# One-column writes behind GpSimd's scatters and gathers, weight bounds cut in four, and a last chunk in halves

## The reference, cut to what matters

```python
mod = (_silu(L0_c) @ L0_wmod).reshape(L0_c.shape[0], 6, 1, -1)
sa, ca, ga, sb, cb, gb = ...            # ga, gb: sign kept, size at least 0.25
h = _layernorm(x) * (1 + ca) + sa
x = x + ga * attention(h)               # linear attention with a memory term, d_mem 32
h = _layernorm(x) * (1 + cb) + sb
x = x + gb * moe(h)                     # 8 experts, top 2, gelu, 128 -> 512 -> 128

def moe(x):
    gate = softmax(flat_x @ w_gate.T)
    topk_scores, topk_idx = top_k(gate, 2)
    h = gelu(einsum('td,edh->teh', flat_x, W1) + b1)
    y = einsum('teh,ehd->ted', h, W2) + b2
    out = einsum('ted,te->td', y, cw)   # cw: the two scores at their experts
```

## Time and profile before

| | |
|---|---|
| median of 3 runs | 661.02 us |
| the profiled execution's own time | 661.97 us |
| its span | 660.2 us |
| busy: PE, DVE, ACT, POOL | 398.8, 446.9, 333.6, 390.6 us |
| scatters (L484), writes of `pause` (L488), gathers (L497) | 128, 128 and 128 |

### The profile page before, as it was taken

The page is one execution under the profiler, slowest core; times in us unless marked ns, Lnnn a source line. Parts: engine busy times, 40 slices in busy tenths (PEclk is TensorE's granted clock), DMA queues, the critical chain, the costliest instruction groups (busy, mean ns, idle before and its releaser), DMA issues. The chain is left out here.

```text
span 660.2 us, 15017 instructions
## 1 busy us (share of the span) xinstructions
PE 398.8 (60%) x4184; PEld 343.1 (52%) x4185; DVE 446.9 (68%) x1035; ACT 333.6 (51%) x746; POOL 390.6 (59%) x472
## 2 busy tenths in 40 slices
PE   5854378467847359999999932200999268962000
PEld 4643366455736238899988922100887157851000
DVE  6788889999887658989978813001798147957323
ACT  2634389669946346666766721000565035549221
POOL 3067000069898899999999978775005725234772
PEclk9966688779768679999999985655799569977555
DMA  8881044525731168644444422211234223425422
GB/s 232 257 298 36 0 122 138 168 86 171 205 98 41 40 177 164 127 119 127 123 113 125 123 60 62 69 52 48 72 95 107 56 60 99 101 58 164 114 60 68
DMA packets 129681, 73.20 MB, mean 111 GB/s; under 512 B 53744, under 2 KB 122992, under 8 KB 129392
## 3 DMA queue, kind: packets, MB, share of 16 engines
q1 hardware_dynamic: 121456, 56.02, 30.9%
q0 software_dynamic: 8192, 16.79, 9.5%
HBM read 21.75 MB, written 34.90 MB: 86 GB/s over the span
## 5 line engine op out<-in xcount | busy, mean ns | idle before, releaser
L497 POOL DMA_INDIRECT ROW<-slot_out,POS x128 | 133.4, 1042 | 130.7 <-DVE X L1007 47.2
L1164 PE MATMUL psA<-WST,ATT 128*128 x2040 | 149.7, 225 | 83.3 <-issue 79.8
L484 POOL DMA_INDIRECT slot_rows<-ROW,POS x128 | 150.7, 1177 | 81.0 <-DVE EXPT L907 59.6
L1164 PEld LDWEIGHTS psA<-WST,ATT 128*128 128x128 f16 x2040 | 130.0, 100 | 98.8 <-issue 90.7
L641 ACT ACTIVATE ATT<-psA,b1T,f_scales 128x256 f32<-128x256 f32 x172 | 83.1, 564 | 121.5 <-remote 82.8
L973 DVE SCALAR_TENSOR_TENSOR ATT<-ATT,f_scales 128x1024 f16<-128x1024 f32 x85 | 109.2, 1284 | 3.0
L982 DVE SCALAR_TENSOR_TENSOR VP<-psA,f_scales,b2B 128x256 f32<-128x256 f32 x85 | 40.9, 481 | 100.2 <-remote 48.1
L971 DVE TENSOR_SCALAR ATT<-ATT,f_scales 128x1024 f16<-128x1024 f32 x85 | 68.1, 802 | 14.2 <-ACT ATT L641 12.1
L641 ACT ACTIVATE ATT<-psV,b1T,f_scales 128x256 f32<-128x256 f32 x84 | 42.9, 561 | 68.4 <-PE psH L1152 29.7
L1152 PE MATMUL psA<-WT,WST 128*128 128x256 f16 x516 | 68.6, 283 | 13.2 <-DMA WT<-slot_rows 6.4
L488 POOL MEMSET pause<- 1x512 f32 x128 | 75.6, 591 | 0.0
(11 more groups left out here) (198 smaller groups left out, 710.7 us busy)
## 6 DMA issues: line engine op xcount, KB each, us to landing
slot_out<-VP SPq DMA_DIRECT2D x85, 128.0 KB
slot_rows<-zero SPq DMA_DIRECT2D x9, 1024.0 KB, 5.4
X<-in_x SPq DMA_DIRECT2D x8, 512.0 KB, 6.8
WST<-in_W SPq DMA_DIRECT2D x2, 2048.0 KB, 14.3
WST<-WT SPq DMA_DIRECT2D x16, 256.0 KB
out<-X SPq DMA_DIRECT2D x16, 256.0 KB
slot_rows<-ROW,POS POOLq DMA_INDIRECT x128
GA<-gate_rows SPq DMA_DIRECT2D x1, 2048.0 KB, 10.7
```

The source lines that it names most:

```text
L484: nc.gpsimd.indirect_dma_start(xg[g], bass.IndirectOffsetOnAxis(ap=POS[:, k * TILES + t:k * TILES + t + 1], axis=0), ROW[:, t * 2 * D:(t + ...
L497: nc.gpsimd.indirect_dma_start(YG[:, o:o + D], None, yg[g], bass.IndirectOffsetOnAxis(ap=POS[:, i:i + 1], axis=0)).then_inc(gathered[c % 2 ...
L1164: last = mm(psD[k % 2][:, h * D:(h + 1) * D], a[:, k % 2, i:i + TOK], W2S[:, ds(e * 2 * FF + b * FF + m * D, D)], start=(m == 0 and c == 0 ...
```

## The change

It has three parts.

1. `pause` has one column instead of 512. The write of it, now in a helper `rest`, stands behind every scatter as before and newly behind each of the 96 gathers of groups 0 and 1. Each write still waits for the one before it. `landed(c-1)` moves from behind the eighth gather of chunk c to behind its third.
2. The bounds of the weights are taken in four pieces: 1024 columns of W1 in step 3 and 1024 columns of W2 in step 4, both ahead of `HL`, and the remaining two times 3072 after step 3, where all of it was. A further small reduction joins the pieces. Six statistics of tiles move from behind step 2 into it, ahead of `HL`.
3. Chunk 15 is gathered so that its first two tiles (4 gathers) come before the other two, each half with a semaphore of its own; DVE mixes and SP stores each half by itself, and no `flag` is written for this chunk.

```diff
-        pause = sb("pause", [1, 512], f32)
+        pause = sb("pause", [1, 1], f32)
...
-            with sp.Fori(0, CHUNKS) as c:
+            with sp.Fori(0, CHUNKS - 1) as c:
                 sp.wait_ge(mixed, c + 1)
                 sp.dma_start(outv[c], ...).then_inc(out_done, 16)
+            for h in range(2):
+                sp.wait_ge(mixed, CHUNKS + h)
+                first = (CHUNKS - 1) * CH + h * CH // 2
+                sp.dma_start(outv[CHUNKS - 1][:, h * CH // 2:(h + 1) * CH // 2, :], ...).then_inc(out_done, 16)
...
+            rests = [0]
+
+            def rest():
+
+                ge(pool, paused, rests[0])
+                nc.gpsimd.memset(pause[:], 0.0).then_inc(paused, 1)
+                rests[0] += 1
...
-                        ge(pool, paused, 2 * t + k)
-                        nc.gpsimd.memset(pause[:], 0.0).then_inc(paused, 1)
+                        rest()
...
-                for k in range(2):
-                    for t in range(CH):
-                        o, i = ((c % YRING) * 2 * CH + k * CH + t) * D, k * TILES + c * CH + t
-                        nc.gpsimd.indirect_dma_start(...).then_inc(gathered[c % 2], 16)
+                for n in range(2 * CH):
+                    if c == CHUNKS - 1:
+                        k, t = n // 2 % 2, n // 4 * 2 + n % 2
+                        done = half_in[n // 4]
+                    else:
+                        k, t = n // CH, n % CH
+                        done = gathered[c % 2]
+                    o, i = ((c % YRING) * 2 * CH + k * CH + t) * D, k * TILES + c * CH + t
+                    nc.gpsimd.indirect_dma_start(...).then_inc(done, 16)
+                    if n == 2 and c:
+                        landed(c - 1)
+                    if g < GROUPS - 1:
+                        rest()
...
                     gather(c, g)
-                    if c:
-                        landed(c - 1)
-            landed(CHUNKS - 1)
...
                 if weights is not None:
                     weights_low(2 * weights[1], weights[0])
+                if beside:
+                    beside()
                 if has(r):
...
-            def weight_bounds():
-
+            def weight_bound(k, n, a, b):
+
+                return nc.vector.tensor_reduce(w_parts[:, k:k + 1], WST[:, n, a:b], AX.X, ALU.max, apply_absolute_value=True)
+
+            EDGE = E * FF // 4
+
+            def first_bound():
                 dve.wait_ge(w_in, 64)
-                for n in range(2):
-                    nc.vector.tensor_reduce(w_bound[:, n:n + 1], WST[:, n, :], AX.X, ALU.max, apply_absolute_value=True)
+                weight_bound(0, 0, 0, EDGE)
+
+            def middle_bounds():
+                weight_bound(1, 0, EDGE, E * FF)
+                weight_bound(2, 1, 0, E * FF - EDGE)
+
+            def last_bound():
+                link(weight_bound(3, 1, E * FF - EDGE, E * FF))
+                nc.vector.tensor_reduce(w_bound[:, 0:2], w_parts[:].rearrange("p (n k) -> p n k", k=2), AX.X, ALU.max)
                 nc.vector.tensor_reduce(w_bound[:, 2:3], b1T[:], AX.X, ALU.max, apply_absolute_value=True).then_inc(wb_ready, 1)
...
-            SECOND_HALF = 40
+            SECOND_HALF, BESIDE = 40, 6
...
-            steps(dve, step, route, {0: second_statistics, 1: bounds_and_tiles, 2: lambda: statistics(2, SECOND_HALF), 3: last_refine, 4: weight_scales}, weights=True)
+            steps(dve, step, route, {0: second_statistics, 1: bounds_and_tiles, 2: lambda: statistics(2, SECOND_HALF + BESIDE), 3: last_refine, 4: weight_scales},
+                  weights=True, beside={2: lambda: tiles(SECOND_HALF, SECOND_HALF + BESIDE), 3: first_bound, 4: last_bound})
...
-            for part in range(4):
-                mix(CHUNKS - 1, CHUNKS - 1 - YRING, part, 3 * MIXED + 2 * (CHUNKS - 1 - MIXED))
+            for h in range(2):
+                mix_half(h, 3 * MIXED + 2 * (CHUNKS - 1 - MIXED) + 3 * h)
```

More of the change, by code:

```diff
@@ L148, in build_adaln_block @@
         b2B = sb("b2B", [128, E * D], f32)
+        w_parts = sb("w_parts", [128, 4], f32)
         w_bound = sb("w_bound", [128, 4], f32)
@@ L214, in build_adaln_block @@
         gathered, scaled = [sem(f"gathered{n}") for n in range(2)], sem("scaled")
+        half_in = [sem(f"half_in{h}") for h in range(2)]
         rows_in, mix_link, mixed, out_done = sem("rows_in"), sem("mix_link"), sem("mixed"), sem("out_done")
@@ L233, in links, with steps @@
             return link
-        def steps(eng, step, route, after={}, weights=False, last=lambda: None):
+        def steps(eng, step, route, after={}, weights=False, last=lambda: None, beside={}):
             for p in range(-1, 5):
-                step(p, p % 2, p // 2, 0)
+                step(p, p % 2, p // 2, 0, **({"beside": beside[p]} if p in beside else {}))
                 after.get(p, lambda: None)()
@@ L415, in _ @@
             outv = A["out"].rearrange("(c t p) d -> c p t d", p=128, t=CH)
-            with sp.Fori(0, CHUNKS) as c:
+            with sp.Fori(0, CHUNKS - 1) as c:
                 sp.wait_ge(mixed, c + 1)
                 sp.dma_start(outv[c], X[:, ds(c * CH * D, CH * D)].rearrange("p (t d) -> p t d", d=D)).then_inc(out_done, 16)
-            sp.wait_ge(out_done, 16 * CHUNKS)
+            for h in range(2):
+                sp.wait_ge(mixed, CHUNKS + h)
+                first = (CHUNKS - 1) * CH + h * CH // 2
+                sp.dma_start(outv[CHUNKS - 1][:, h * CH // 2:(h + 1) * CH // 2, :],
+                             X[:, first * D:(first + CH // 2) * D].rearrange("p (t d) -> p t d", d=D)).then_inc(out_done, 16)
+            sp.wait_ge(out_done, 16 * (CHUNKS + 1))
             for k in range(RING):
@@ L765, in weights_low, with step @@
                                                    op1=ALU.subtract).then_inc(ws_low, 1)
-            def step(p, j, half, g, weights=None):
+            def step(p, j, half, g, weights=None, beside=None):
                 q, r = p - 1, p - 2
@@ L1014, in _, with mix_half @@
                         mix(c, c - first // YRING * YRING, part, 3 * MIXED + 2 * (c - MIXED) - 1, True)
-            for part in range(4):
-                mix(CHUNKS - 1, CHUNKS - 1 - YRING, part, 3 * MIXED + 2 * (CHUNKS - 1 - MIXED))
+            def mix_half(h, base):
+                c, t = CHUNKS - 1, CH // 2
+                first = c * CH + h * t
+                y = YG[:, (c - YRING) * 2 * CH * D:(c - YRING + 1) * 2 * CH * D].rearrange(
+                    "p (k h t d) -> p k h t d", k=2, h=2, t=t)[:, :, h]
+                dve.wait_ge(half_in[h], 16 * CH)
+                cw = CW[:, :, first:first + t].rearrange("p k (t o) -> p k t o", o=1).broadcast_to([128, 2, t, D])
+                nc.vector.tensor_tensor(y, y, cw, ALU.mult).then_inc(mix_link, 1)
+                dve.wait_ge(mix_link, base + 1)
+                nc.vector.tensor_tensor(y[:, 0], y[:, 0], y[:, 1], ALU.add).then_inc(mix_link, 1)
+                dve.wait_ge(mix_link, base + 2)
+                gb = GA[:, (2 * c + h) * D:(2 * c + h + 1) * D].rearrange("p (o d) -> p o d", o=1).broadcast_to([128, t, D])
+                nc.vector.tensor_tensor(y[:, 0], y[:, 0], gb, ALU.mult).then_inc(mix_link, 1)
+                dve.wait_ge(mix_link, base + 3)
+                x = X[:, first * D:(first + t) * D].rearrange("p (t d) -> p t d", d=D)
+                nc.vector.tensor_tensor(x, x, y[:, 0], ALU.add).then_inc(mixed, 1)
+            for h in range(2):
+                mix_half(h, 3 * MIXED + 2 * (CHUNKS - 1 - MIXED) + 3 * h)
         @block.tensor
```

8 lines of the change are left out of this document (4 added, 4 removed).

## The result

The changed kernel takes 783.65 us (median of 3 runs, 780.10 to 785.24) against 661.02: a ratio of 1.185, 95% interval 1.177 to 1.192. It is slower by 18.5%. The forecast was 544 us; what came is the rival (b), whose sum was 809.

The account below looks back on a forecast made before the run. Bound: scatters set when gathers start, gathers freeze the experts, whose end sets the last 32 gathers. Experts end at 472 us, 96 gathers at 490, group 2's at 536; the tail makes 542.4, plus 1.8: 544 us, range 527 to 569.

Parts of the forecast that it names:

- rival (b): Scatter stage from 133 us: lost spacing lets scatters freeze attention (71 us) and experts (91 us) too; 809 us, chance 0.12.
- the part on the freeze: Experts beside gathers: one-column writes end the freeze by holding GpSimd's queue to one operation ahead; experts end at 472 us.
- Rival (a): Gathers beside experts: writes don't end the freeze, scatters stay clean; 121 us frozen, 647 us; chance 0.17 with partial forms.
- The Trainium skill's rule: Gathers: only the next write waits, never a gather, so gathers could follow as close as before and the freeze stay; 647 us.
- Bounds: Weight bounds ahead of the scatters: pieces and moved statistics save 2.9 us; group 0's scatters start at 133.0 us.
- GpSimd's maximum: In the bounds, from about 78.3 to 81.8 us: could cost 0 to 5.2 us, taken as 0.
- Scatters: 1.34 us each in group 0, 1.67 beside the experts; the last out at 323 us, not 383.
- Gathers: Groups 0 and 1, from 337 us: 1.65 us each with its write beside experts, between 1.26 and 2.12.
- End: Behind the experts' end at 472 us: gathers left until 490, group 2's 32 in 46.2 us, then 1.5, 2.0 and 2.9 us.

Follow-up runs that it names:

- long_both: Changed kernel with `pause` of 512 columns behind scatters and gathers: 608.46 us, ratio 0.918.
- depth4: Changed kernel with 512-column writes, each into another of four places and waiting for the write four before it: 608.26 us, ratio 0.923.
- three_short: Changed kernel with three one-column writes, each waiting for the one before, where it has one: 607.95 us, ratio 0.919.
- long_scatter: Changed kernel with 512 columns behind scatters and one behind gathers: 654.71 us, ratio 0.988.
- burst4: Changed kernel with a write of 1536 columns behind every fourth indexed DMA only: 603.40 us, ratio 0.915.
- only_bounds_halves: Kernel before with only the bounds in four pieces and chunk 15 in halves, 512 columns behind scatters, nothing behind gathers: 657.99 us, ratio 0.993.

## Why the prediction was wrong

**The step that failed** is in the part on the freeze: the write "holds GpSimd's queue to one operation ahead ... I take it that the second is what counts". The first counts, the spacing: scatters 1.26 us apart froze attention and cost the 123 us, and at 1.65 us (long_both) nothing froze. The queue depth plays no part (depth4), nor does the length of the write (three_short), nor that something stands between two DMAs (long_scatter, and burst4 from the other side).

The reason that I gave, that the hole outlasts the DMA traffic by 4 us, does not speak for depth at all: something that fills up while DMAs follow closely, and drains slowly, outlasts them too, and fits that a pause after four helps. It is not a backlog of the DMAs' data. In the changed kernel the last gather before a wait ends its row at 560.16 us; the DMA engines stop moving data in the next two microseconds, and PE is held until 563.78:

```profile
561.00:562.00 1.00, 0.26 (x1) 0.09 (x1) 0.00 (x0) 0.00 (x0) 0.00 (x0) 0.50 0.07 21
562.00:563.00 1.00, 0.00 (x0) 0.10 (x1) 0.00 (x0) 0.00 (x0) 0.00 (x0) 0.50 0.00 0
```

In the packets of the same trace the last data of a scatter inside the first freeze mostly ends 0.91 us behind the scatter's row, for the 10th as for the 55th. Nor do the DMAs fill it alone: in long_scatter 14 had gone out, most of them 1.25 us apart, and PE still did 43 matmuls before it froze, so the other engines' own instructions seem to take part. What fills up stays open. The Trainium skill says in "Perfetto Trace Analysis", section "DMA Instruction — SWDGE (GPSIMD)", that the row of such a DMA ends when the descriptors are generated, not when the data has moved. The trace agrees: behind the last gather GpSimd waited 1.46 us for its data.

There was a hint in the earlier trace rows that I priced at 0.12: freezes at 1.25 to 1.45, none at 1.66 and more, and nothing in between. With two explanations that fit all rows, the edit that keeps the one and gives up the other deserved near even chances.

**Rival (b)** had the mechanism, and its size nearly. It summed 71 us of freeze in attention and 91 in the experts. The holes were 70 us (141 to 211) in attention for group 0, about 55 for group 1, whose scatters from 253 us on now also met attention, and some 40 for group 2 in the experts: 165 in all against 162. Its time of 809 us was 25 too long all the same: the holes are not empty (PE worked 9.82 of 44 us in the first), and what else is in the 25 us I did not work out. The reason against it, that the port conflicts would space scatters to 1.67 beside the experts, failed because frozen engines make no conflicts: distances in the holes were mostly 1.26.

**Rival (a)** alone is long_scatter, 654.7 us against 647. **The Trainium skill's rule** that only what waits on the semaphore is gated ("GPSIMD Engine Reference", section 2.1) agrees with this trace: gathers with a write between them go at 1.26 us, without at 1.25.

**Bounds.** The first scatter was forecast at 133.0; it is at 131.99 in the changed kernel and at 132.8 on average over the 15 kernels with these bounds, 135.93 and 136.10 without. GpSimd's maximum started at 77.54 us and took 0.71, and cost nothing, as taken.

**Scatters.** 1.34 forecast in attention; undisturbed they came at 1.26, on average over group 0 at 1.40 (131.99 to 208.83). The forecast changed the old average of 1.72, which holds disturbed scatters too; from the old undisturbed distance, 0.97 + 0.52 + 0.17 = 1.66, it would have been 1.28. **Gathers** at 1.65 beside the experts: never seen, as the experts stood still.

**End.** Forecast from the last gather's end to the span's end 6.4 us, measured 6.4 (772.01 to 778.4); 32 gathers of group 2 46.2, measured 46.7 (725.31 to 772.01). These terms were right, and only_bounds_halves adds that the halves alone would have brought none of it.

## What to carry to other kernels

A delay that looks like waste may be a rate limiter: before it is shortened, vary it in steps (512, 256, 128) and read what the other engines do per microsecond. Indexed DMAs from GpSimd should here keep a mean distance of about 1.7 us while other engines work; one pause per four costs fewer GpSimd instructions than one behind each, and behind the last work of the other engines no pause is needed. Where two explanations fit every row, take the chances from that, not from the one with the better story.

## What was not expected of the hardware

- Indexed DMAs of 128 rows at a mean distance below about 1.6 us take the issue of instructions from PE, DVE and ACT: 262 matmuls were left of some 335 at 1.56 us, 144 at 1.43, 53 at 1.32 undisturbed and 30 at 1.26, with the DMA engines 13 to 24% busy in the changed kernel's holes in attention. What the engines wait for inside the chip no row shows; this stays open. All these times come from traced executions; whether the freeze is there without a trace no run shows.
- The number of rows (64 or 128) and their bytes (256 or 512) don't matter for it; the DMAs do.
- Scatters and gathers act alike.
- A one-element write of GpSimd took 0.095 us on average in attention and 0.18 beside the experts, one of 512 elements 0.52 and 0.66.
